# Cross-attention over 25088 context tokens: two context tiles weighed in one stretch, rounded keys stacked by way of HBM

## The reference

```
q = (layernorm(x) @ Wq.T) * 32 ** -0.5       # 256 x 512, split into 16 heads of 32
k = context @ Wk.T ; v = context @ Wv.T      # 25088 x 512
scores = sigmoid(q . k) per head             # 16 x 256 x 25088, no softmax
o = (scores . v) @ Wo.T ; x = x + o
```

## Time and profile before

| What | Value |
|---|---|
| Median of 3 runs | 2120.65 us |
| Profiled execution, span | 2119.5 us |
| PE busy | 2096.5 us (99%) |
| ACT busy | 1361.7 us (64%) |
| DVE busy | 1190.9 us (56%) |
| POOL busy | 1022.3 us (48%) |
| DMA, mean | 74 GB/s |

### The profile page before, as it was taken

How to read it: one execution, slowest core, us unless ns; L and a number is a source line. 1 busy time by engine, 2 the same in 40 slices (tenths; PEclk the granted TensorE clock), 3 DMA queues, 4 the chain that set the end, 5 groups by cost and what they waited for, 6 DMA issues and landing times. The chain is left out here.

```text
span 2119.5 us, 42205 instructions
## 1 busy us (share of the span) xinstructions
PE 2096.5 (99%) x15810; PEld 1632.6 (77%) x15812; DVE 1190.9 (56%) x1495; ACT 1361.7 (64%) x1702; POOL 1022.3 (48%) x900
## 2 busy tenths in 40 slices
PE   9999999999999999999999999999999999988999
PEld 6777777777777777777777777777777777746998
DVE  6656556565565665656556565565655656525422
ACT  7666666666666666666666666666666666632764
POOL 5066564665646656466564665646656460000000
PEclk9999999999999999999999999999999999999999
DMA  5111211112111121111211112111121110122774
GB/s 179 42 60 40 74 45 61 58 40 74 45 61 57 40 74 45 62 57 40 74 45 63 56 40 74 45 63 56 40 74 45 63 56 21 65 101 112 277 278 168
DMA packets 43908, 157.09 MB, mean 74 GB/s; under 512 B 5600, under 2 KB 5600, under 8 KB 31200
## 3 DMA queue, kind: packets, MB, share of 16 engines
q1 hardware_dynamic: 43872, 156.59, 20.5%
HBM read 154.47 MB, written 0.52 MB: 73 GB/s over the span
## 5 line engine op out<-in xcount | busy, mean ns | idle before, releaser
L302 ACT ACTIVATE probs<-sc 128x1024 f32<-128x1024 f32 x784 | 761.6, 1022 | 371.5 <-PE sc L463 366.8
L352 DVE TENSOR_TENSOR k_stack<-kp,k_stack 32x512 fp32r<-32x512 f32 x772 | 529.5, 686 | 720.0 <-ACT k_stack L295 701.8
L295 ACT ACTIVATE k_stack<-kp 32x512 fp32r<-32x512 f32 x772 | 456.3, 591 | 257.4 <-PE kp L443 243.2
L267 POOL TENSOR_TENSOR piece_hi<-piece,zero 128x512 fp32r<-128x512 f32 x176 | 220.1, 1251 | 666.6 <-DMA piece<-w_all_dram 642.6
L463 PEld LDWEIGHTS sc<-rows_r,k_stack 96*128 96x128 f32 x3136 | 413.2, 190 | 100.0 <-issue 83.6
L463 PE MATMUL sc<-rows_r,k_stack 96*128 96x256 f32 x3136 | 460.1, 289 | 0.9 <-DMA k_stack<-k_stack 0.9
L454 PE MATMUL vp<-weights_r,c_hi 128*128 128x512 f32 x1568 | 392.9, 392 | 0.0
L443 PE MATMUL kp<-c_hi,weights_r 128*128 128x512 f32 x1544 | 386.8, 392 | 0.0
L474 PE MATMUL acc<-probs,v 128*32 128x256 f32 x6272 | 381.3, 382 | 0.1
L454 PEld LDWEIGHTS vp<-weights_r,c_hi 128*128 128x128 f32 x1568 | 282.0, 189 | 51.2 <-issue 0.8
L443 PEld LDWEIGHTS kp<-c_hi,weights_r 128*128 128x128 f32 x1544 | 277.2, 188 | 49.8
(11 more groups left out here) (135 smaller groups left out, 882.8 us busy)
## 6 DMA issues: line engine op xcount, KB each, us to landing
ctx_raw<-ctxT_dram SPq DMA_DIRECT2D x49, 1024.0 KB, 4.8
piece<-w_all_dram SPq DMA_DIRECT2D x178, 256.0 KB, 4.7
w_raw<-w_all_dram SPq DMA_DIRECT2D x44, 1024.0 KB, 4.8
weights<-wqk_dram SPq DMA_DIRECT2D x2, 1024.0 KB, 6.1
probs<-wqT_dram SPq DMA_DIRECT2D x1, 1024.0 KB, 6.0
probs<-wkT_dram SPq DMA_DIRECT2D x1, 1024.0 KB, 8.0
probs<-wvT_dram SPq DMA_DIRECT2D x1, 1024.0 KB, 11.9
k_stack<-k_stack SPq DMA_DIRECT2D x4, 256.0 KB, 3.0
```

The costliest lines, as they stand in the source:

```text
L267: nc.gpsimd.tensor_tensor(piece_hi[:], piece[:, t % 2, :], zero[:].to_broadcast([P, PIECE]), ALU.add).then_inc(piece_rounded, 1)
L295: nc.scalar.activation(kst[0:D, par, j, g, :], source[D * j:D * (j + 1), :], ACT.Copy).then_inc(k_hi, 1)
L302: nc.scalar.activation(probs[:, t % 2, g, :], sc[g % 2][:], ACT.Sigmoid).then_inc(probs_ready, 1)
L352: nc.vector.tensor_tensor(kst[D:2 * D, par, j, g, :], source[D * j:D * (j + 1), :], f32(kst[0:D, par, j, g, :]), ALU.subtract).then_inc(k_ ...
```

## The change

1. **Order on PE.** The values of a tile are made in the tile itself, behind scores 3, and no longer a tile ahead. The weighing of an even tile is put off: behind the values of every odd tile both tiles are weighed, 8 groups in one stretch. `last_chunk` is gone; the last chunk runs in the common order, without keys. In chunk 0 the values of tile 0 stand behind scores 3.
2. **The key stack.** ACT rounds all 128 rows of `kp` at once into `kr_hi` (`k_round`), DVE takes the difference into `kr_lo` (`k_difference`). SP stores both to a scratch `kept` in HBM, with heads and rows exchanged, waits for the landing, and loads from there: `hi` into the first and third block, `lo` into the second. Each group has a semaphore `k_stacked[g]`, for which PE waits before the first scores of that group in the next chunk. The stack's layout changes from head, group to group, head. Chunk 0's own keys are stacked as before.
3. **Waits and places.** `kp` is free once `kr_lo` is made (`k_split`), and `kr_hi`, `kr_lo` are free once their stores have landed. `split_chunk` on DVE moves to the end of the chunk, the load that waits for it on SP too; the loads of pieces are put one into each tile, between the stores and the loads of the stack. PE's wait for the split chunk is divided into one for `hi` and one for `lo`.

```diff
-        kst = sb("k_stack", [P, 2, HG, G, CH], F32R)
+        kst = sb("k_stack", [P, 2, G, HG, CH], F32R)
+        kr_hi, kr_lo = sb("k_rows_hi", [P, CH], F32R), sb("k_rows_lo", [P, CH], F32R)
...
             def one(c, par, first, k_next, split_next, load_next, looped):      # SP
-                if load_next:
-                    sp.wait_ge(ctx_split, c + 3)
-                    sp.dma_start(raw[:], ctxT[c + 3]).then_inc(ctx_loaded, 16)
-                if looped:
-
-                    for n in range(2, TC + 2):
+                for t in range(TC):
+                    if k_next:
+                        sp.wait_ge(k_rounded, c * TC + (t + 1))
+                        sp.dma_start(kept[t, 0].rearrange("d j n -> j d n"), f32(kr_hi[:])).then_inc(k_hi_kept, 16)
+                        sp.wait_ge(k_split, c * TC + (t + 1))
+                        sp.dma_start(kept[t, 1].rearrange("d j n -> j d n"), f32(kr_lo[:])).then_inc(k_lo_kept, 16)
+                    if looped:
+                        n = t + 2
                         u = c - 1 if n < TC else c % UNITS
                         sp.wait_ge(piece_used, c * TC + (n - 2 - TC + 1))
                         sp.dma_start(piece[:, n % 2, :], w_all[u][:, n % TC * PIECE:(n % TC + 1) * PIECE]
                                      ).then_inc(piece_loaded[n % 2], 16)
+                    if k_next:
+                        to = f32(kst[:, 1 - par, t, :, :])
+                        sp.wait_ge(k_hi_kept, c * (TC * 16) + (t + 1) * 16)
+                        sp.dma_start(to[0:D], kept[t, 0]).then_inc(k_stacked[t], 16)
+                        sp.dma_start(to[2 * D:3 * D], kept[t, 0]).then_inc(k_stacked[t], 16)
+                        sp.wait_ge(k_lo_kept, c * (TC * 16) + (t + 1) * 16)
+                        sp.dma_start(to[D:2 * D], kept[t, 1]).then_inc(k_stacked[t], 16)
+                if load_next:
+                    sp.wait_ge(ctx_split, c + 3)
+                    sp.dma_start(raw[:], ctxT[c + 3]).then_inc(ctx_loaded, 16)
...
+            def k_round(c, t):                                                  # ACT
+                act.wait_ge(k_made, c * TC + (t + TC + 1))
+                if not (isinstance(c, int) and c == 0 and t == 0):
+                    act.wait_ge(k_hi_kept, c * (TC * 16) + t * 16)
+                nc.scalar.activation(kr_hi[:], kp[:], ACT.Copy).then_inc(k_rounded, 1)
...
                     if k_next:
-                        k_rows(tile + TC, 1 - par, t, kp[:])
+                        k_round(c, t)
...
+            def k_difference(c, t):                                             # DVE
+                dve.wait_ge(k_rounded, c * TC + (t + 1))
+                if not (isinstance(c, int) and c == 0 and t == 0):
+                    dve.wait_ge(k_lo_kept, c * (TC * 16) + t * 16)
+                nc.vector.tensor_tensor(kr_lo[:], kp[:], f32(kr_hi[:]), ALU.subtract).then_inc(k_split, 1)
...
                 for t in range(TC):
-                    tile = c * TC + t
-                    if t == TC - 1 and split_next:
-                        dve.wait_ge(v_made, tile + 1)
-                        split_chunk(c + 2, par)
                     if k_next:
-                        k_rest(tile + TC, 1 - par, t, kp[:])
-                    if k_next or t < TC - 1:
-                        v_out(tile + 1, (t + 1) % 2, not (first and t == 0))
+                        k_difference(c, t)
+                    v_out(c * TC + t, t % 2, not (first and t < 2))
+                if split_next:
+                    split_chunk(c + 2, par)
...
             def one(c, par, first, k_next, split_next, load_next, looped):      # PE
                 for t in range(TC):
                     tile = c * TC + t
+                    opening = first and t == 0
                     for g in (0, 1):
-                        if first and t == 0:
+                        if opening:
                             first_stack(g)
-                        scores(tile * G + g, par, t, g, not (first and t == 0))
...
+                        elif t == 0:
+                            pe.wait_ge(k_stacked[g], c * STACKED)
+                        scores(tile * G + g, par, t, g, not opening)
+                    if k_next:
+                        chunk_ready = ()
+                        if t == 0:
+                            chunk_ready = (((ctx_hi, c + 2),), (), ((ctx_split, c + 2),))
+                        if not opening:
+                            pe.wait_ge(k_split, tile)
+                        k_project(1 - par, t, kp[:], before=chunk_ready or ((), (), ()))
+                    if opening:
                         zero_sums()
                     for g in (2, 3):
...
                         scores(tile * G + g, par, t, g, True)
-                    ahead = t + 1 if t < TC - 1 else 0
-                    v_project(tile + 1, par if ahead else 1 - par, ahead, True)
-                    for g in range(G):
-                        weigh(tile, t, g)
+                    if opening:
+                        pe.wait_ge(wv_split, 1)
+                    v_project(tile, par, t, not opening)
+                    if t % 2:
+                        for done in (t - 1, t):
+                            for g in range(G):
+                                weigh(c * TC + done, done, g)
...
+        kept = nc.dram_tensor("k_rows", (G, 2, D, HG, CH), F32, kind="Internal").ap()
```

More of the change, by code:

```diff
@@ L100, in keep_clock, with cross_attention @@
         nc.tensor.matmul(to, zeros[:, 0:P], zeros[:], start=True, stop=True, skip_group_check=True)
-def cross_attention(nc, x, ctxT, wqT, wkT, wvT, woT, wqk, wv, bv, wo, w_all, keep):
+def cross_attention(nc, x, ctxT, wqT, wkT, wvT, woT, wqk, wv, bv, wo, w_all, kept, keep):
     ident, x1, qst, next_weights = keep["ident"], keep["x1"], keep["rows"][0], keep["weights"][1]
@@ L155, in cross_attention @@
         ctx_hi, ctx_split = sem("ctx_hi"), sem("ctx_split")
-        k_made, k_hi, k_lo, k_dup = sem("k_made"), sem("k_hi"), sem("k_lo"), sem("k_dup")
+        k_made, k_hi, k_lo = sem("k_made"), sem("k_hi"), sem("k_lo")
+        k_rounded, k_split = sem("k_rounded"), sem("k_split")
+        k_hi_kept, k_lo_kept = sem("k_hi_kept"), sem("k_lo_kept")
+        k_stacked = [sem(f"k_stacked{g}") for g in range(G)]
         k_dup0 = [sem(f"k_dup_of_first{g}") for g in range(G)]
@@ L166, in cross_attention @@
         SCALE = float(D) ** -0.5
+        STACKED = 3 * 16
         def q_of(j):
@@ L207, in _ @@
                 sp.wait_ge(k_hi, (g + 1) * HG)
-                sp.dma_start(f32(kst[2 * D:3 * D, 0, :, g, :]), f32(kst[0:D, 0, :, g, :])).then_inc(k_dup0[g], 16)
+                sp.dma_start(f32(kst[2 * D:3 * D, 0, g, :, :]), f32(kst[0:D, 0, g, :, :])).then_inc(k_dup0[g], 16)
             sp.wait_ge(ctx_split, 2)
@@ L432, in _, with k_project @@
             last.then_inc(q_made, 1)
-            def k_project(u, par, g, to, free, before=((), (), ())):
-                if free:
-                    pe.wait_ge(k_lo, u * HG)
+            def k_project(par, g, to, before=((), (), ())):
                 n = 0
@@ L478, in weigh @@
                     last.then_inc(probs_used, 1)
-            k_project(0, 0, 0, k_first[0], False, before=(
+            k_project(0, 0, k_first[0], before=(
                 ((wk_hi_done, 1), (ctx_hi, 1)), ((wk_split, 1),), ((ctx_split, 1),)))
             for g in range(1, G):
-                k_project(g, 0, g, k_first[g], False)
+                k_project(0, g, k_first[g])
             pe.wait_ge(q_lo, HG)
@@ L498, in zero_sums @@
                                      skip_group_check=True)
[L500 to L513, removed]
@@ L1106, in build @@
         keep["v"] = rows[:, 2, :, :].rearrange("p g l -> p (g l)").rearrange("p (a n) -> p a n", a=LT)
-        cross_attention(nc, x, ctxT, wqT, wkT, wvT, woT, wqk, wv, bv, wo, w_all, keep)
+        kept = nc.dram_tensor("k_rows", (G, 2, D, HG, CH), F32, kind="Internal").ap()
+        cross_attention(nc, x, ctxT, wqT, wkT, wvT, woT, wqk, wv, bv, wo, w_all, kept, keep)
         keep |= {"any_inexact": sb("any_inexact", [1, 1], mybir.dt.int32), "inexact_ready": sem("any_inexact_ready"),
```

21 lines of the change are left out of this document (6 added, 15 removed).

## The result

The changed kernel takes 2436.4 us (median of 4, 2435.1 to 2437.6), where the kernel before took 2120.8 beside it: 1.149 of the time before, 95% interval 1.148 to 1.151. The prediction, 2092.5 with a range to 2126, has the wrong sign and misses by 344 us.

The account below looks back on a forecast made before the run. PE was taken as the bound, at 2.4 GHz. Fewer weighing stretches -30.7, opening +1.85, last chunk +0.7, key stack 0: -28.15 on 2119.5 is 2091.35, median 2092.5 us; own range 2086 to 2100, full range 2085 to 2126.

Parts of the forecast that it names:

- the way of the last group's keys: Tile 3's keys through rounding, stores and loads to the next chunk's tile 0: 7.5 to 9.2 us, inside 11.5.
- The key stack by HBM (the condition): Stacking keys through HBM delays PE nowhere if the last group's stack is in time: cost 0.
- The landing of the store: Key store to HBM, priced like the 256 KB output: 2.0 us; 4.2 if spread over four engines alone.
- The backlog: Four engines carrying 9.4 us of work in a 9.3 us tile: about 1 us added to the last group's way.
- rival A: Stores on few engines make PE wait for k_stacked[3] in tile 0 of 48 chunks: 2150 to 2193 us; chance 0.21.
- The main term of 96 x 0.32: Chunks 0 to 47 have 96 fewer weighing stretches on PE, each saving 0.32 us: 30.7 us less.
- The sum: All terms together: -28.15 us on the profiled span of 2119.5, giving a median of 2092.5 us.
- The opening: Chunk 0's start, keys now ahead of tile 0's values: PE reaches the next scores at 38.45, cost 1.85 us.
- The last chunk: Without keys between them, scores 2 and 3 wait for ACT: the chunk takes 31.3 us, cost 0.7.
- The work of ACT and DVE is worth nothing by itself: In the loop PE is the bound, so relieving ACT (1.8 us a tile) and DVE saves no time.
- rival C: A weighing stretch pays 0.14 again at its second tile, or the pay is waits on probs: 14.7 less, 2106; with B 0.17.
- The spare: Time left over in the last group's 11.5 us before PE needs its stack: 2.3 to 4 us.

Follow-up runs that it names:

- after: The changed kernel itself, as profiled, with both edits and stores of outermost size 4, against the kernel before: 2436.4 us, ratio 1.149.
- half: Changed kernel without the stores of kr_lo; the stack's middle block is loaded from the rounded rows instead: 2283.5 us, ratio 1.077 to the kernel before.
- clock: Changed kernel with 20 dummy matmuls into vp ahead of the wait for the last group's stack, once a chunk: 2335.3 us, ratio 1.101 to the kernel before.
- store16: Changed kernel with the scratch written as 128 rows, the loads exchanging heads and rows: 2093.6 us, ratio 0.988 to the kernel before.
- old_order: Kernel before, its PE order kept, with the key stack by HBM in store16's layout: 2233.9 us, ratio 1.053 to the kernel before.
- pair: Changed kernel's PE order alone, keys stacked by ACT and DVE as in the kernel before, no scratch: 2190.1 us, ratio 1.033 to the kernel before.
- old_late: old_order with the chunk's split, and with it the context load, moved behind the last tile: 2196.1 us, ratio 1.037 to the kernel before.
- store8: Changed kernel with an unused scratch row after every 16, so stores have outermost size 8, and six loads a stack: 2355.2 us, ratio 1.111 to the kernel before.

## Why the prediction was wrong

**The step that failed** is the way of the last group's keys, in "The key stack by HBM (the condition)". It was taken at 0, with 2.1 us a chunk as its upper end; it costs 7.1 (343 / 48): 4.8 of lateness and 2.3 of clock. Three terms in it were mis-sized or absent.

- The landing of the store. The forecast used the output's 2.0 us, a DMA of another form; the prediction itself said that no row shows an outer 4. On four engines it put 4.2: 1.3 for all but the transfer, and 2.9 of transfer. Measured are 6.0 (1018.45 to 1024.49 in after) and 6.5 (half). The transfer was right, 256 KB at 102 GB/s is 2.6; the rest is 3.4, not 1.3. By this alone hi lands at 6.7, lo 2.6 to 2.9 behind it, and a load of 3.4 to 4 more makes 13: late before any backlog.
- The queue of SP. Its waits are in order, so tile 3's first store can't be issued until tile 2's second has landed: at 2.8 and not at 0.7. The backlog was priced at 1 us as bytes on engines; it came as a blocked issuer, and with `kr_lo` not yet free. 16.4 against 11.5 is the 4.9 measured. (Tile 3's keys follow tile 2's by 0.96 + 2.75 + 0.96 + 2.75 = 7.4, and not by the 7.6 of the prediction; the trace of after has 7.41.)
- The clock. No term of the sum held what a wait does to the matmuls behind it: 2.35 us a chunk by the trace of after, 113 us in all, of which 101 came back in clock.

The mechanism had been named as rival A, with its place, its sign in the waits and its point of decision (0.59 us a chunk), and given 0.21. Its price was 1.2 to 2.1 us a chunk, 2150 to 2193; even the rival was short by more than 240 us. The prediction's own count had the four engines full, 9.4 of 9.3 us a tile, and its main sum still took 0. The form of the store spoke for A by itself: the rule that names four engines was weighed, and then priced with a start that belongs to 16.

**What was right**, shown by store16, where the condition holds. The main term of 96 x 0.32: the stretch of 64 at 3.59 and the pair at 18.60. The sum: 2092.5 predicted, 2093.6 measured. The opening: 38.45 predicted for the next scores, 38.60 in after, 38.73 in store16. The last chunk: 31.3 predicted, 31.7 in store16, from 1816.82 to DVE's copy at 1848.52. The work of ACT and DVE is worth nothing by itself: 9.46 a tile in old_order. So rival C is out: the switch is paid once a stretch. The spare, though, was not 2.3 to 4 us in store16. There ACT starts rounding tile 3 at 1028.51 and the third load is issued at 1032.53 and lands 5.8 later, 9.8 us of the 11.5 gone. Over the 48 chunks the way takes 7.9 to 10.6, so the spare can be as little as 0.9.

**What the prediction didn't say.** Each half of the change is a loss without the other, as far as was run: the order alone is 70 us slower than before (pair), the way through HBM alone 76 to 114 us slower (old_late and old_order, each with a wait of its own that better placing might remove). The prediction worked out that ACT fits in the 3.7 us with one rounding of 0.61, but it took the light rounding for granted; pair shows that this is the condition on which the longer stretch rests, and that it is worth 96 us there.

**Open.** How much of store8's 261 us over store16 belongs to its store and how much to its six loads; why a store on few engines starts or ends 1 to 2 us later beyond its transfer (only that it does is shown); and what a second `kr_lo` buffer, or another queue for the stores, would give back of the 2.1 us by which tile 3's first store is issued late.

## What to carry to other kernels

Before a DMA is priced by a row of the trace, compare its outermost size with that row's and not just its bytes: a store laid out so that 16 divides the outermost size cost 2.3 us here, with 4 outermost 6.0. Where the consumer's slack is of the order of two such landings, follow the issuing queue through its in-order waits, not the bytes, and add to a wait of TensorE what the lower clock behind it costs: 2.3 us here behind waits of 4.6. Two edits made together may each be the other's condition: price each one without the other before you call one of them free.

## What the runs showed of the hardware

A 256 KB store from SBUF to HBM took 2.3 us to land with an outermost size of 128 (2.0 in old_order and old_late), 2.5 with 32 and gaps, 4.1 with 8 (6.3 in tile 3), and 6.0 to 6.5 with 4 (6.2 to 7.2 in tile 3). At 22.5 GB/s for one engine the transfer is 0.7, 0.7, 1.5 and 2.9 of it, so the remainder grows too: 1.6, 1.8, 2.6 and over 3. While little but stores with 4 was under way, 0.26 of the 16 engines were busy.

The third load of tile 3's stack, 256 KB, landed in 6.7 us in old_late and in 7.8 in old_order (medians of 48), where a 1 MB load was issued 0.7 us behind it: a later neighbour delays an earlier transfer.

TensorE's granted clock was 0.51 in the 4.6 us behind a wait of 3.97 us (after), and 1.00 at the same place when dummy matmuls covered all but 0.94 of the wait (clock).
